# A selective-scan block with a binary MLP on one core: normalised tokens kept from the first stage, and work moved from VectorE and ScalarE

## What is computed

```python
xn = _layernorm(x)
# branch 1: a selective scan block on xn
normed = rmsnorm(xn, input_norm_w)
x_z, z = split(normed @ in_proj_W)            # 256 and 256 features
xc = silu(conv4(x_z) + conv_b)                # 4 taps along the tokens
dt = clip(softplus(xc @ dt_W + dt_b), 0.001, 0.1)
Bp, Cp = xc @ B_W, xc @ C_W                   # 64 each
h = exp(dt * A) * h + dt * Bp * xc            # a state of 256 x 64 per sequence, token after token
y = (h . Cp) * silu(z)
x1 = xn + y @ out_proj_W
n2 = rmsnorm(x1, ffn_norm_w)
attn = x1 + (silu(n2 @ gate_W) * (n2 @ up_W)) @ down_W
# branch 2: a binary MLP on xn, weights +1 or -1
h1 = relu(s0 * [xn, -xn] @ K0) * 2            # 512
h2 = relu(s1 * h1 @ K1) * 2                   # 512
out = x + attn + s2 * h2 @ K2
```

## Time and profile before

| what | us |
|---|---|
| median of 3 runs | 1169.29 (1166.89 to 1173.1) |
| the profiled execution | 1161.89 |
| its span, from the first to the last instruction | 1160.1 |
| busy: PE, DVE, ACT, POOL | 1013.9, 936.7, 910.1, 845.2 |
| mean granted TensorE clock | 0.907 of full speed |

### The profile page before, as it was taken

How to read it: one execution, slowest core, us unless ns; L and a number is a source line. 1 busy time by engine, 2 the same in 40 slices (tenths; PEclk the granted TensorE clock), 3 DMA queues, 4 the chain that set the end, 5 groups by cost and what they waited for, 6 DMA issues and landing times.

```text
span 1160.1 us, 27892 instructions
## 1 busy us (share of the span) xinstructions
PE 1013.9 (87%) x8006; PEld 435.1 (38%) x8006; DVE 936.7 (81%) x2130; ACT 910.1 (78%) x1093; POOL 845.2 (73%) x1215
## 2 busy tenths in 40 slices
PE   5988865699999989897999986999998898899997
PEld 3656521123434333333343332434343333243436
DVE  5667645788989889896999976879897899698983
ACT  1775684888989889886999886879897999788971
POOL 5465405687888878786888875778787888688880
PEclk9999985558989999998999988889899899798999
DMA  4243469999999999998999997989999899999940
GB/s 134 105 147 130 172 226 294 326 319 316 315 317 334 321 327 329 319 330 303 304 347 324 334 306 281 320 270 345 318 341 331 305 337 327 286 328 323 334 154 10
DMA packets 77140, 327.38 MB, mean 282 GB/s; under 512 B 13856, under 2 KB 33184, under 8 KB 41888
## 3 DMA queue, kind: packets, MB, share of 16 engines
q1 hardware_dynamic: 76960, 325.31, 83.0%
HBM read 303.24 MB, written 22.02 MB: 280 GB/s over the span
## 4 chain that ended last, share of the span: by engine, by line
PE 33%; DVE 23%; POOL 14%; issue 14%; DMA 8%; ACT 4%; SPq 3%; DVEq 1%; ACTq 0%; POOLq 0%
PE ps L793 11%; POOL decayed L588 9%; DVE ps L1215 8%; PE ps L738 7%; DMA decay<-dt_stage 7%; PE ps L878 6%; DVE state L1226 6%; PE ps L892 4%; DVE h L1330 2%; ACT state L1025 2%; SPq L392 1%; DVE soft L1142 1%; POOL soft L539 1%; DVE h L1339 1%; SPq L190 1%
## 5 line engine op out<-in xcount | busy, mean ns | idle before, releaser
L588 POOL TENSOR_TENSOR decayed<-decay,state 128x256 f32<-128x256 f32 x1024 | 726.3, 733 | 215.6 <-DVE state L1226 172.6
L1005 ACT ACTIVATE decay<-decay,a_col 128x2048 f32<-128x2048 f32 x256 | 512.6, 2003 | 65.8 <-DMA decay<-dt_stage 52.0
L1226 DVE TENSOR_TENSOR state<-decayed,ps 128x256 f32<-128x256 f32 x1024 | 399.8, 417 | 62.6 <-POOL decayed L588 31.8
L1215 DVE TENSOR_TENSOR ps<-decay,ps 128x512 f32<-128x512 f32 x512 | 352.7, 689 | 73.9 <-ACT state L1025 33.9
L793 PE MATMUL ps<-state,c_cols 128*32 128x256 f32 x4096 | 362.3, 429 | 0.0
L1025 ACT COPY state<-ps 128x512 f32<-128x512 f32 x512 | 289.0, 581 | 91.0 <-issue 47.6
L738 PE MATMUL ps<-moving,b_rows 36*128 36x256 bf16 x1024 | 214.9, 293 | 98.1 <-DVE ps L1215 94.1
L745 PE MATMUL ps<-moving,b_rows 36*128 36x256 bf16 x1024 | 216.0, 294 | 13.7 <-DMA b_rows<-b_stage 13.7
L878 PE MATMUL ps<-h,w 128*128 128x256 f32 x512 | 188.6, 456 | 1.0 <-DVE h L1330 0.8
L738 PEld LDWEIGHTS ps<-moving,b_rows 36*128 36x128 bf16 x1024 | 58.8, 96 | 286.8 <-DVE ps L1215 169.1
L793 PEld LDWEIGHTS ps<-state,c_cols 128*32 128x32 f32 x4096 | 84.2, 112 | 122.9 <-issue 104.6
(11 more groups left out here) (122 smaller groups left out, 823.7 us busy)
## 6 DMA issues: line engine op xcount, KB each, us to landing
decay<-dt_stage SPq DMA_DIRECT2D x512, 512.0 KB, 7.1
moving<-u_stage SPq DMA_DIRECT2D x64, 288.0 KB
b_stage<-b_parts SPq DMA_DIRECT2D x24, 384.0 KB, 3.8
b_rows<-b_stage SPq DMA_DIRECT2D x128, 72.0 KB
dt_stage<-dt_tok SPq DMA_DIRECT2D x8, 512.0 KB, 3.1
u_stage<-u_parts SPq DMA_DIRECT2D x8, 512.0 KB, 3.1
x_tok<-in_L_attn_x_dram SPq DMA_DIRECT2D x4, 512.0 KB, 3.6
u_stage<-u_parts SPq DMA_DIRECT2D x8, 256.0 KB, 2.1
```

The source lines that it names most:

```text
L588: nc.gpsimd.tensor_tensor(decayed[:, p], decay[:, dec_slot(m, k), p, k % TS, :], state[:, (k - 1) % RING, p * E:(p + 1) * E], ALU.mult).th ...
L1005: nc.scalar.activation(pair, pair, ACT.Exp, scale=a_col[:, 2:3]).then_inc(decay_ready, 1)
L1215: nc.vector.tensor_tensor(ps[:, acc_bank(m, k), :].rearrange("p (q e) -> p q e", q=HQ), decay[:, dec_slot(m, k), HQ:Q, k % TS, :], ps[:, a ...
L1226: nc.vector.tensor_tensor(state[:, k % RING, p * E:(p + 1) * E], decayed[:, p], ps[:, SELFP + k % 2, p * E:(p + 1) * E], ALU.add).then_inc ...
```

## The change

The normalised tokens xn are made once, in the first stage: GpSimd writes them behind its `norms` (four `tensor_scalar` a sequence, from the mean and 1/std that are there), SP stores them to a new DRAM tensor `xn_stage` and loads them for each group beside x. The moments, sums, pow, shift and xn of the groups are gone. `place_c` and n2 move from ScalarE to GpSimd (n2 as one instruction), the second relu from VectorE to ScalarE in two pieces of 128x512. `silu_z` is laid out by chunk, and `gated` becomes one instruction. The final sums of PE start a step later in four parts instead of five. In the scan's chunk layout the numbers are TC = 16, GT = 2.

```diff
-        silu_z = sb("silu_z", [P, EH, B, T])
+        silu_z = sb("silu_z", [P, EH, NC, B, TC])
...
-        K_STATS, K_MOMENTS, K_RSTD_SUM, K_RSTD, K_SHIFT, K_XN, K_XN_T, K_XN_FEAT = -7, -6, -5, -4, -2, 0, 2, 3
-        K_Y_T, K_GATED, K_OUT, K_X1, K_SQUARE, K_RRMS_SUM, K_RRMS, K_BASE, K_N2 = 6, (7, 8), 9, 11, 12, 13, 15, 12, 17
+        K_XN_T, K_XN_FEAT = 2, 3
+        K_Y_T, K_GATED, K_OUT, K_X1, K_SQUARE, K_RRMS_SUM, K_RRMS, K_BASE, K_N2 = 6, 8, 9, 11, 12, 13, 15, 12, 17
...
-        K_H2, K_H2_RELU = (14, 24), ((22, 23), (32,))
-        K_LAST, K_RESULT = 33, 38
-        H2_STEPS, LAST_STEPS = 8, 5
+        K_H2, K_H2_RELU = (14, 24), (23, 32)
+        K_LAST, K_RESULT = 34, 38
+        H2_STEPS, LAST_STEPS = 8, 4
...
+                def store_xn(n):
+
+                    wait_all(sp, [(S["xnorm_ready"], n + 1)])
+                    sp.dma_start(xn_stage[n:n + 1].rearrange("o (p j) d -> p o (j d)", j=NJ),
+                                 xnorm[:].rearrange("p j d -> p (j d)").unsqueeze(1)).then_inc(S["xn_stored"], 16)
...
+                    if n + 2 < B:
+                        store_xn(n + 2)
...
+                    for j in range(GT):
+                        sp.dma_start(xn[:, j, :], xn_stage[:, bass.ds(g * TG + j * TC, TC), :]
+                                     ).then_inc(G["f_xn_loaded"], 16)
...
                     nc.gpsimd.tensor_tensor(nrm[:, 5], nrm[:, 4], nrm[:, 1], ALU.mult).then_inc(S["rms_ready"], 1)
+                    after(pool, "xn_stored", n, per=16, back=1)
+                    for j in range(NJ):
+                        m = nc.gpsimd.tensor_scalar(xnorm[:, j], x_tok[:, n % XB, j], mean_var[:, bb, j, 0:1],
+                                                    nrm[:, 1, j:j + 1], ALU.subtract, ALU.mult)
+                    m.then_inc(S["xnorm_ready"], 1)
...
+                def place_c(chunk, cb):
+
+                    for bb in range(2):
+                        m = nc.gpsimd.tensor_tensor(
+                            c_cols[:, cb, :, bb * TC:bb * TC + (TC - 1) * (2 * TC + 1) + 1:2 * TC + 1],
+                            cb_feat[:, bb, :, bass.ds(chunk * TC, TC)], parity[:, bb:bb + 1].unsqueeze(1).broadcast_to([P, Q, TC]), ALU.mult)
+                    m.then_inc(c_placed, 1)
...
+                    if k == K_N2:
+                        after(pool, "f_rrms_ready", g)
+                        after(pool, "f_n2_t_ready", g, back=1)
+                        nc.gpsimd.tensor_tensor(n2[:], x1[:], f_nrm[:, 1].unsqueeze(2).broadcast_to([P, GT, D]), ALU.mult
+                                                ).then_inc(G["f_n2_ready"], 1)
...
+                pool.wait_ge(start_zeroed, 1)
+                pool.wait_ge(S["c_ready"], B)
+                place_c(0, 0)
                 chunks(pool, step)
...
+                    for r in range(2):
+                        if k == K_H2_RELU[r]:
+                            act.wait_ge(G["f_h2_proj"], g * 2 + r + 1)
+                            nc.scalar.activation(h2[:, 2 * r:2 * r + 2, :].rearrange("p c t -> p (c t)"), ps[:, FB, :],
+                                                 ACT.Relu, scale=s_fold[:, 0:1]).then_inc(G["f_h2_ready"], 1)
...
+                    if k == K_GATED:
+                        after(dve, "f_y_t_ready", g)
+                        after(dve, "f_proj_ready", g, back=1)
+                        nc.vector.tensor_tensor(
+                            gated[:], ps[:, FA, :].rearrange("e (h t) -> e h t", h=EH),
+                            silu_z[:, :, bass.ds(g * GT, GT)].rearrange("e h c b t -> e h (c b t)"), ALU.mult
+                        ).then_inc(G["f_gated_ready"], 1)
```

More of the change, by code:

```diff
@@ L807, in finish @@
                     if k == K_XN_T:
-                        after(pe, "f_xn_ready", g)
+                        pe.wait_ge(G["f_xn_loaded"], (g + 1) * (16 * GT))
                         after(pe, "f_hid_ready", g, back=1)
@@ L1079, in moments @@
                     dve.wait_ge(x_loaded[n // 2], 16)
+                    after(dve, "xnorm_ready", n, back=2)
                     for j in range(NJ):
@@ L1260, in finish @@
                 def finish(g, k):
-                    if k == K_STATS:
-                        dve.wait_ge(G["f_x_loaded"], (g + 1) * (16 * GT))
-                        after(dve, "f_rstd_ready", g, back=1)
-                        for j in range(GT):
-                            m = nc.vector.bn_stats(f_stats[:, j], x_in[:, j])
-                        m.then_inc(G["f_stats_ready"], 1)
-                    if k == K_MOMENTS:
-                        after(dve, "f_stats_ready", g)
-                        nc.vector.memset(wait_mark[:], 0.0)
-                        for j in range(GT):
-                            m = nc.vector.bn_aggr(f_mv[:, j], f_stats[:, j])
-                        m.then_inc(G["f_mv_ready"], 1)
-                    if k == K_SHIFT:
-                        after(dve, "f_rstd_ready", g)
-                        after(dve, "f_xn_ready", g, back=1)
-                        nc.vector.scalar_tensor_tensor(f_nrm[:, 4], f_mv[:, :, 0], -1.0, f_nrm[:, 1], ALU.mult, ALU.mult
-                                                       ).then_inc(G["f_shift_ready"], 1)
                     if k == K_XN_FEAT:
```

89 lines of the change are left out of this document (22 added, 67 removed).

## The result

The changed kernel takes 1192.31 us (1191.21 to 1199.16, 4 runs) beside 1170.72 us for the kernel before, a ratio of 1.0195 with a 95% interval of 1.0152 to 1.0238. Measured again beside two of its variants it gave 1.0243 [1.0174, 1.0312]. It is slower by 23 to 28 us (1% is 11.7 us here), where no change was forecast, and it lies 2 us above the upper end of the range, 1190. A ratio is estimated from the runs of both kernels without those more than 1.5% above the fastest of the same kernel, so it is not quite the quotient of the medians, which are over all runs.

A forecast was written before the change was run, and what follows sets the result against it. Interlocked engines (about 55 us a round) and transfers (about 56) were taken to bound the scan. Terms +7, +3, -8, -0.5 and +0.7 gave +2.2 us: 1164.1 profiled, 1171.5 us as median, range 1154 to 1190.

The forecast's parts named there:

- Reloading xn in the scan: Scan: 32 more 64 KB loads, 6.3 us of DMA time, half of it counted: +3 us, bounds 0 and +6.5.
- The limit of a round: Scan: engines allow about 55 us a round, transfers about 56; the round at 900.3 us took 55.0 at DMA share 0.93.
- the room was 58 us in all: Scan: 960 us less 902 us of DMA work; faster engines help only until transfers are the limit.
- First stage: Four more GpSimd instructions a batch, 0.40 us each, ahead of u_rest, delay the first stage: +7 us, bounds +2 and +15.
- The lock between GpSimd and VectorE: First stage: VectorE's SBUF-to-SBUF instructions do not run while a GpSimd instruction does, so added GpSimd work costs VectorE too.
- Engines: Scan: relief of 2.2 us a round less 1.1 on GpSimd, half of it counted: -8 us, bounds 0 and -33.
- steps 11 to 17: Scan round: GpSimd already the limit there; its added work makes this stretch 1.1 us longer, bounds 0.3 and 2.5.
- The store: First stage: eight 256 KB transfers from SP, issued well before GpSimd waits for them: cost 0.
- rival 4: First stage: xnorm's store stuck behind u_split, GpSimd waiting up to 2 us in each of 7 batches: 1186 us, chance 0.05.
- Rival 3: GpSimd becomes the limit in steps 11 to 17 and the first stage: +19, 1188.5 us, chance 0.29.
- Rival 2: Scan: the engines' relief comes through, 33 us gained: 1146 us, or 1158 with two thirds; chance 0.26.
- the signals named: Right: first scan step 5 to 9 us later, scan 4 to 8 us shorter; wrong: first stage over 12 us longer.

The follow-up runs named there:

- x loaded once: Kernel before without 30 of its 32 loads of x, all groups using the first group's tokens: 1143.65 us, ratio 0.9831.
- change without tokens: Whole change without the normalised tokens, groups taking their own moments and xn as before: 1162.61 us, ratio 0.9957; measured again 0.9926.
- tiny loads: Kernel before with 32 added loads, each shrunk to one row of 512 B, at the spare loads' place: 1165.69 us, ratio 1.0014.
- spare loads early: Kernel before with the 32 added loads of 64 KB issued near step 6 of a round, not step 13: 1181.68 us, ratio 1.0158.
- spare loads: Kernel before with 32 added loads of 64 KB into an unread tile, at the place of the xn loads: 1185.25 us, ratio 1.0167.
- one wide load: Kernel before with the same 2.1 MB of added loads as 16 transfers with rows of 1 KB: 1184.66 us, ratio 1.0208.
- the two orders of GpSimd: Changed kernel unaltered, 1193.40 us, beside the same with the four xnorm instructions at the end of GpSimd's first-stage slot, 1185.71 us.
- the tokens last: Changed kernel with the four xnorm instructions at the end of GpSimd's first-stage slot, behind u_parts: 1184.73 us, ratio 1.0188; measured again 1.0121.

## Why the prediction was wrong

**Reloading xn in the scan, +3 us with bounds 0 and +6.5: this step failed.** Loads of the same bytes cost +19 us alone, +24 in the shape of wide rows, +18 at another place, and leaving as many out gave -20 us. The upper bound was the loads' own time in the ring, as if a late transfer delayed the end by no more than itself. What the runs showed in its place, each row's last three columns from one profiled execution:

| kernel | ratio | wait for decay, us | landing, us | rounds with clock 0.90 or lower, of 13 |
|---|---|---|---|---|
| x loaded once | 0.9831 | 27.6 | 6.6 | 3 |
| change without tokens | 0.9957 | 53.6 | 7.4 | 4 |
| before | 1 | 52.0 | 7.1 | 2 |
| tiny loads | 1.0014 | 46.6 | 6.9 | 6 |
| spare loads early | 1.0158 | 78.6 | 8.0 | 4 |
| spare loads | 1.0167 | 82.1 | 8.3 | 7 |
| after | 1.0195 | 70.1 | 7.7 | 7 |
| one wide load | 1.0208 | 61.1 | 7.6 | 7 |

ScalarE's waits moved by 9 to 32 us for 6.3 us of transfers. Two executions of one kernel differ by some 6 us in this (70.1 and 76.0 for the kernel after), so the direction is clear and the sizes are not. Read with the full rounds: the ring carries each round's bytes with about 1 us to spare, so a transfer that is held up makes the decay tiles behind it late, and there is little room to catch up.

A further step suggests itself: PE idles for the late tile, its granted clock falls from 2.4 towards 1.2 GHz, and PE then limits at 0.80 with the ring at 0.84, which loses room that the next rounds need. The Trainium skill, "TensorE: Matmul & The Clock Gate", HAM oscillation, describes a loop whose waits for DMA bring the clock down again and again. Rounds at 0.80 to 0.86 do occur here, but the runs speak against them as the multiplier. Tiny loads have 6 rounds at a low clock and no loss, the early spare loads 4 and 18 us of loss, and at equal mean clock the bytes still cost 16 us. As an estimate, in the 108 runs of the kernel before beside the experiments 0.01 of granted clock goes with 7.7 us, and the three kernels with spare loads had median clocks of 0.887 to 0.892 for its 0.898: 5 to 8 of their 18 to 24 us could be the clock. No run held it still. So that added bytes cost about three times their own time is shown; what multiplies them stays open.

**The limit of a round.** "The interlocked engines allow a round of about 55 us, and the transfers about 56" was half wrong. The 0.93 share of the round at 900.3 us misled me: the other 55.0 us round ran at 0.98, one of 54.1 us in the kernel with tiny loads at 0.98 too, and with VectorE 2 us lighter the shortest was 54.6 us. I had said that the room was 58 us in all, and still priced loads at half their ring time.

**First stage, +7 us with bounds +2 and +15.** It came to +13.5, within the bounds and at twice the term. Mis-sized was the instruction: 0.80 us at its usual and 0.92 in the mean, not 0.40, above the upper bound of 0.74 that the 128x256 row gave. Mis-sized too was the reach: the four slots between norms gave 7.3 us, near the 6.5 for five, but the slots ahead of them gave 2.4 us, not 0.5, and the last batch's four instructions came through whole, with 4 us. A row that I did not use held the way out: GpSimd idles 4.3 us ahead of a slot's norms, and the new work was put behind that idle time instead of into it. The lock between GpSimd and VectorE was seen right: `normed` fell from 2.89 to 1.17 us.

**Engines, -8 us.** The size was right: -5 and -9 measured. Its working is borne out in part. VectorE's busy time fell by 1.9 to 2.2 us a round, where I had priced 3.3, with 2.2 of it on the path; how much was on the path no run shows. GpSimd's instructions cost what I took or less, but steps 11 to 17 did not grow by 1.1 us a round: from the scan's first VectorE instruction of step 11 to that of step 18 it is 11.9 us at the least in both kernels, and 13.4 for 12.9 us in the mean of 13 rounds. So part of the agreement is luck.

**The store, 0.** Right, but for one wait of 2.0 us, so rival 4 fell. **Rival 3** gave nearly the right time, 1188.5, for the wrong reason: C's columns took 314 ns, GpSimd was busy 47.6 us in the best round both before and after, and its moves alone gave 0.9965. **Rival 2** fell: the moved work gave 5 to 9 of its 33 us. The ring isn't the only reason, since with 30 loads of x left out the same moves gave 11. Of the signals named, a first stage longer by over 12 us and more than 39 us of waits for the decay came true; the four rows of 0.4 us, a shorter scan and a DMA share of 0.95 did not.

The sum with the measured terms: +13.5 for the first stage, +18 to +24 for the bytes, -5 to -9 for the moved work, or +22 to +33, against +23 and +28 measured. The 13.5 us are the trace's; between the medians of the two orders of GpSimd only 7.7 came through.

## What to carry to other kernels

Where the DMA share of whole rounds is 0.98 and the consumers already wait for loads, price added bytes at several times their own transfer time (about three here), or measure them with spare loads into an unread tile, before trading work on an engine for a reload. Keeping a value "in memory" is a saving only if the ring has room for fetching it. When work is added to an engine in a pipeline slot, look for its longest idle time and put the work there: the same four instructions delayed the scan by 13.5 us in one place of the slot and by under 1 us in another. Before a count of slow rounds or a low clock is called the cause of a loss, count it in a kernel that has no loss.

## What the runs showed of the hardware

- Added or removed transfers of 2 MB (0.6% of 327 MB) moved the time by 1.6 to 2.1%, in either direction, whether in rows of 512 B or of 1 KB, while 32 transfers of one 512 B row each moved it by 0.14%, which can't be told from nothing.
- GpSimd's `tensor_scalar` of 128x128 with two per-partition operands takes 0.79 us at the least, more than its two-input 128x256 (614 to 739 ns in the mean). Behind `u_parts` the first of four took 2.1 us, ending 1.0 us after VectorE's `soft` had ended, and the others 0.79. All 32 in the kernel with the tokens last (ns minimum/median/maximum):

```profile
L551 POOL TENSOR_SCALAR xnorm<-x_tok,mean_var,nrm x32: 787/792/2208, 9.4 to 128.5; 128x128 f32<-128x128 f32 x32
```

- The same 8006 matmuls kept PE busy for 1013.9 us at a mean granted clock of 0.907 and for 1033.9 us at 0.880. The kernel before alone, in 108 runs, took from 1154.88 to 1186.78 us at mean clocks of 0.913 to 0.879, the longer times mostly at the lower clocks. A busy time that grows with no new instruction shows a lower clock, not why it is low.
